# One attention and mixture-of-experts layer: chunk work spread over more units, expert results added in DRAM, experts moved from unit 38 to 44

## The reference

```
xn  = layernorm(x)                                     # 4096 tokens x 128
q, k, v = xn @ Wq + bq, xn @ Wk + bk, xn @ Wv + bv     # 16 heads of 8
attn = softmax(q k^T / sqrt(8)) v, per batch and head
logits = xn @ router_w.T                               # 8 experts
g = sigmoid(top 2 logits) / their sum
ffn = sum over the 2 chosen experts e of g_e * (silu(xn @ w_gate[e]) * (xn @ w_up[e])) @ w_down[e]
out = x + attn @ Wo + bo + ffn
```

## Time and profile before

| | |
|---|---|
| median of 3 runs | 1033.23 us (1033.08 to 1034.17) |
| the profiled execution | 1033.09 us, its span 1031.3 us |
| PE busy | 906.4 us (88%) |
| DVE busy | 684.9 us (66%), 610.4 of them in the 512 reductions of L736 |
| ACT busy | 680.3 us (66%), 538.9 of them in the exponentials of L499 |
| POOL busy | 419.3 us (41%) |
| granted clock of PE, mean | 0.894 |

### The profile page before, as it was taken

The page is one execution under the profiler, slowest core; times in us unless marked ns, Lnnn a source line. Parts: engine busy times, 40 slices in busy tenths (PEclk is TensorE's granted clock), DMA queues, the critical chain, the costliest instruction groups (busy, mean ns, idle before and its releaser), DMA issues.

```text
span 1031.3 us, 17126 instructions
## 1 busy us (share of the span) xinstructions
PE 906.4 (88%) x5469; PEld 411.0 (40%) x5469; DVE 684.9 (66%) x807; ACT 680.3 (66%) x1452; POOL 419.3 (41%) x639
## 2 busy tenths in 40 slices
PE   6275598994879999999999999999999999999870
PEld 5142233331434454444444454444444544333220
DVE  6145588883377767777777767777777677888100
ACT  2040356773448877888877887778887788787630
POOL 8454004774153222323222222222232223288786
PEclk8595558996569999999999999999999999999875
DMA  4359301233222223333333332333332222133234
GB/s 125 92 154 278 126 22 48 74 108 105 64 58 62 82 71 97 82 84 84 83 104 84 83 84 84 83 84 86 83 84 86 79 80 72 47 38 38 34 53 85
DMA packets 99354, 86.84 MB, mean 84 GB/s; under 512 B 13496, under 2 KB 86848, under 8 KB 99264
## 3 DMA queue, kind: packets, MB, share of 16 engines
q1 hardware_dynamic: 85968, 72.21, 25.2%
q0 software_dynamic: 12560, 13.39, 5.9%
q10 hardware_dynamic: 736, 0.14, 0.1%
HBM read 58.68 MB, written 26.49 MB: 83 GB/s over the span
## 4 chain that ended last, share of the span: by engine, by line
PE 67%; POOL 10%; issue 7%; ACT 6%; DVE 5%; DMA 2%; SPq 2%; POOLq 0%; ACTq 0%; DVEq 0%
PE ps L896 21%; PE ps L879 20%; PE ps L868 9%; PE ps L933 7%; POOL slots L385 6%; ACT probs L499 5%; PE ps L919 5%; POOL x_sb L423 3%; PE ps L909 2%; POOL probs L361 1%; DVE maxima L736 1%; PE ps L923 1%; DMA qk<-m_rows 1%; DVE m_parts L746 1%; DVE attn L759 1%
## 5 line engine op out<-in xcount | busy, mean ns | idle before, releaser
L736 DVE TENSOR_REDUCE maxima<-ps 128x1 f32<-128x1024 f32 x512 | 610.4, 1221 | 251.7 <-PE ps L879 250.7
L499 ACT ACTIVATE probs<-ps 128x512 f32<-128x512 f32 x1024 | 538.9, 604 | 150.8 <-PE ps L868 150.6
L868 PE MATMUL ps<-qk 36*128 36x512 f32 x1024 | 399.0, 475 | 31.0 <-DMA qk<-m_rows 18.7
L879 PE MATMUL ps<-qk 34*128 34x512 f32 x1024 | 356.9, 457 | 31.6 <-issue 22.6
L896 PE MATMUL ps<-probs,v_all 128*9 128x512 f32 x2048 | 286.9, 635 | 0.0
L879 PEld LDWEIGHTS ps<-qk 34*128 34x128 f32 x1024 | 166.1, 197 | 254.7 <-DVE maxima L736 135.2
L403 POOL TENSOR_TENSOR gxu<-gu 128x256 f32<-128x256 f32 x72 | 52.5, 730 | 419.8 <-ACT gu L535 419.8
L868 PEld LDWEIGHTS ps<-qk 36*128 36x128 f32 x1024 | 171.6, 194 | 112.1 <-ACT probs L499 85.1
L423 POOL DMA_INDIRECT x_sb<-results,slot x64 | 99.2, 1549 | 34.1 <-issue 18.0
L385 POOL DMA_INDIRECT slots<-x_sb,slot x64 | 61.4, 960 | 89.2 <-DVE x_sb L730 70.0
L933 PE MATMUL ps<-xg_T,gu_w 128*128 128x128 f32 x576 | 83.6, 290 | 0.1
(11 more groups left out here) (124 smaller groups left out, 463.0 us busy)
## 6 DMA issues: line engine op xcount, KB each, us to landing
gu_w<-L_ffn_w_gate SPq DMA_DIRECT2D x72, 128.0 KB, 2.1
gu_w<-L_ffn_w_up SPq DMA_DIRECT2D x72, 128.0 KB, 2.2
dn_w<-L_ffn_w_down SPq DMA_DIRECT2D x72, 128.0 KB, 2.1
qk<-q_parts SPq DMA_DIRECT2D x128, 64.0 KB, 2.7
qk<-k_parts SPq DMA_DIRECT2D x128, 64.0 KB, 2.7
k_parts<-probs SPq DMA_DIRECT2D x24, 256.0 KB, 3.2
slots<-y_acc POOLq DMA_DIRECT2D x9, 528.0 KB, 11.4
xg<-slots SPq DMA_DIRECT2D x72, 66.0 KB, 2.1
```

Of the source, the lines that this page charges most:

```text
L499: act.activation(probs[:, u % NPB, q, h, :], ps[:, s_bank(j), :], ACT.Exp).then_inc(s_read, 1)
L736: dve.tensor_reduce(maxima[:, p % 2, qt, h:h + 1], ps[:, x_bank(i):x_bank(i) + 2, :].rearrange("p a k -> p (a k)"), AX.X, ALU.max, negate= ...
L868: pe.matmul(ps[:, bank, :], t[r, 1, kt * P:(kt + 1) * P], t[r, 0, q * CH:(q + 1) * CH], start=True, stop=True).then_inc(s_filled, 1)
L879: mm = pe.matmul(ps[:, x_bank(i) + k, :], t[r, 0, qt * P:(qt + 1) * P], t[r, 1, k * CH:(k + 1) * CH], start=True, stop=True)
```

## The change

- Expert results: `store_result`, the 64 gathers and POOL's sums go. A DRAM tensor `acc` of 128 + 4096 rows is filled with x by two SP DMAs at unit 4. The scattered rows carry a fifth extra column with their row number in `acc` (XW 132 to 133). After `hidden(t)` POOL adds tile t - 1 to `acc` with one accumulating indirect DMA, each waiting for the one before it to land. At the end SP loads `acc` in 4 DMAs into `x_sb`, DVE adds the output bias (in units 252 to 255) and adds it to `y_acc`. The reload of x and the bias addition on POOL go.
- Chunks: the staging tiles `qk_st`, `hi_st`, `lo_st` are their own, and ACT's wait for all stores goes. `xnT` holds all chunks. Turns of chunks 2 to 7 stand in units -11 to -6, each with the logits of its chunk two steps later; q, k and v of a chunk take two units (q of chunk 7 in unit -1, its k and v in unit 0). All these jobs share the three score-side banks. The lower parts of chunks 0 and 1 are DVE's, and the norms of chunks 2 to 7 are ACT's.
- SP issues `load_pair` of pairs 0 to 2 ahead of chunk 2's stores, pair 3 at unit 0. POOL issues the zeroing of the slots as soon as pair 0 has landed.
- Routing takes units -4 to 7, its ranks are taken after unit 0.
- Experts: cluster c stands in unit 44 + 11c/4, the last in unit 244.

```diff
-FF0 = 38
+FF0 = 44
-    return FF0 + 5 * c // 2
+    return FF0 + 11 * c // 4
+for _c in REST:
+    for _job, _step in (("turn", 4 * (_c - 2)), ("lg", 4 * (_c - 2) + 2), ("q", 8 * (_c - 2) + 3), ("k", 8 * (_c - 2) + 5),
+                        ("v", 8 * (_c - 2) + 7)):
+        CHUNK_AT.setdefault((_step // 4 - LX, _step % 4), []).append((_job, _c))
+UPPER_AT = {2 * (c - 2) + 1 - LX: c for c in REST}
+LOGITS_AT = NC - 2 - LX
+ROUTE_AT = {r - 4: r for r in range(12)}
+SUM_AT = {U - 4 + b: b for b in range(B)}
+RANKS_AT = 0
...
+            for p in range(NQ - 1):
+                load_pair(p)
             for u in UNITS:
-                if u >= KT and u % KT == 0 and u // KT + NQ - 1 < NP:
+                if u - 1 in UPPER_AT:
+                    store_parts(UPPER_AT[u - 1])
+                if u >= 0 and u % KT == 0 and u // KT + NQ - 1 < NP:
                     load_pair(u // KT + NQ - 1)
+                if u == 4:
+                    sp.dma_start(acc_dram[P:P + T, :], x.rearrange("b s e -> (b s) e")).then_inc(acc_set, 16)
+                    sp.dma_start(acc_dram[0:P, :], x[0, 0:P, :]).then_inc(acc_set, 16)
...
+            pool.wait_ge(qk_in[0], LOADS)
             pool.wait_ge(zeros_ready, 1)
             for k in range(TILES // 8):
                 pool.dma_start(pieces[k], zeros).then_inc(zeros_stored, 16)
+            for c in REST:
+                lower(c)
...
+            def add_result(t):
+                pool.wait_ge(s_read, s_full("rows", t + 2))
+                if t == 0:
+                    pool.wait_ge(acc_set, 32)
+                else:
+                    pool.wait_ge(added, 16 * t)
+                pool.indirect_dma_start(out=acc_dram, out_offset=bass.IndirectOffsetOnAxis(ap=ids[:, t % 4:t % 4 + 1], axis=0),
+                                        in_=result[:, t % 3, :], in_offset=None, compute_op=ALU.add).then_inc(added, 16)
             for t in range(TILES):
                 gate_of(t)
                 hidden(t)
+                if t >= 1:
+                    add_result(t - 1)
+            add_result(TILES - 1)
...
-            upper(0)
-            dve.wait_ge(std_ready, 2)
-            dve.reciprocal(mom[:, 1, NT // B:NT], mom[:, 4, NT // B:NT]).then_inc(rstd_ready, 2)
-            upper(1)
+            statistics(1)
+            upper(0)
+            statistics(2)
+            upper(1)
+            statistics(3)
...
-                if u == 0:
-                    for c in range(NC):
-                        act.wait_ge(parts_stored[c], 80)
```

More of the change, by code:

```diff
@@ L126, in build @@
         probs = sb("probs", [P, NPB, 2, 2, CH])
[L127 to L130, removed]
+        qk_st, hi_st, lo_st = (sb(n, [P, 2, 2, CH]) for n in ("qk_st", "hi_st", "lo_st"))
         gu_w = sb("gu_w", [P, 2, 2, F])
@@ L325, in _ @@
             n = NT // B
+            sp.wait_ge(added, 16 * TILES)
+            for b in range(B):
+                sp.dma_start(x_sb[:, b * n:(b + 1) * n, 0:E],
+                             acc_dram[P + b * S:P + (b + 1) * S, :].rearrange("(m p) e -> p m e", p=P)).then_inc(acc_in[b], 16)
             for b in range(B - 1):
@@ L470, in take_chunk, with norm, take_turn @@
-            def take_chunk(c):
-                s = c % 2
+            def norm(c):
+                if c == REST[0]:
+                    act.wait_ge(rstd_ready, 2)
+                for j in range(TPC):
+                    n = c * TPC + j
+                    act.activation(x_sb[:, n, 0:E], x_sb[:, n, 0:E], ACT.Identity, scale=mom[:, 1, n:n + 1],
+                                   bias=mom[:, 5, n:n + 1]).then_inc(xn_rest, 1)
+            def take_turn(c):
+                j = S_NO["turn", c]
+                act.wait_ge(s_filled, j + 1)
+                act.activation(xnT[:, c, :], ps[:, s_bank(j), :], ACT.Copy).then_inc(s_read, 1)
@@ L562, in _ @@
                 for n, (_, _, h, q) in enumerate(STEPS):
+                    for job in CHUNK_AT.get((u, n), ()):
+                        take_chunk_job(*job)
                     if n == 2 and u in CL_AT:
@@ new lines, in turn_norm, with project, project_v @@
+                bank = s_room(S_NO["turn", c])
+                for j in range(TPC):
+                    mm = pe.transpose(ps[:, bank, j * P:(j + 1) * P], x_sb[:, c * TPC + j, 0:E], ident[:, :])
+                mm.then_inc(s_filled, 1)
+            def project(job, c, weights):
+                pe.wait_ge(s_read, s_full("turn", c))
+                bank = s_room(S_NO[job, c])
+                pe.matmul(ps[:, bank, :], weights[:, :], xnT[:, c, :], start=True, stop=True).then_inc(s_filled, 1)
+            def project_v(c):
+                bank = s_room(S_NO["v", c])
+                for j in range(TPC):
+                    mm = pe.matmul(ps[:, bank, j * E:(j + 1) * E], xnT[:, c, j * P:(j + 1) * P], wv[:, :], start=True, stop=True)
+                mm.then_inc(s_filled, 1)
@@ new lines, in logits, with chunk_job @@
+            def logits(c):
+                pe.wait_ge(s_read, s_full("turn", c))
+                for n in range(c * TPC, (c + 1) * TPC):
+                    mm = pe.matmul(ps[:, 7, n * NE:(n + 1) * NE], xnT[:, c, (n - c * TPC) * P:(n - c * TPC + 1) * P], rw_cols[:, :],
+                                   start=True, stop=True)
+                mm.then_inc(lg_ps, 1)
+            def chunk_job(job, c):
+                if job == "turn":
+                    turn_norm(c)
+                if job == "lg":
+                    logits(c)
+                if job == "q":
+                    project("q", c, wq)
+                if job == "k":
+                    project("k", c, wk)
+                if job == "v":
+                    project_v(c)
```

258 lines of the change are left out of this document (115 added, 143 removed).

## The result

The kernel after takes 973.05 us (median of four runs, 971.94 to 1033.59; the kernel before in the same session 1033.7). The ratio is 0.9407, with a 95% interval of 0.9388 to 0.9425. So it is faster by 6%, where 10% was forecast, and 931 with its range up to 955 missed it. The profiled execution took 972.98 us with a span of 971.3. It is compared with the profiled 1033.09 of before, whose span is 1031.3.

A forecast was written before the change was run, and what follows sets the result against it. Stages had different limits: DVE paced plain units at 2.76 us, PE added 1.52 per cluster. Savings 12.0 + 32.1 + 36.5 + 23.9 = 104.5 off 1033.09 gave 928.6, plus 2.4 for DMA: 931 us (0.76), range 914 to 955.

The forecast's parts named there:

- Start, -12.0: Up to the first reduction: chunk 1's last store at 23.4, first reduction at 33.5 instead of 45.48; 12.0 us saved.
- Units -11 to 12, -32.1: Chunk and routing units: 28 us for seven units, then 49.4 and 13.8; 91.2 instead of 123.35 us.
- Units -4 to 7, 49.4: Routing units: DVE sets the pace with reductions, routing parts, upper parts and ranks, 49.4 us in all.
- Units 8 to 12, 13.8: Units after the routing: five at 2.76 us each, 13.8 us.
- Experts' start, -36.5: Units 37 on: scatters end near 194, before unit 42 at 205, so PE's stall, half clock and POOL's addition go; 36.5 us saved.
- The adds, cost 0: Expert stage: accumulating DMAs land in 3.3 us, their chain needs 3.6 of 9.1 us per tile; no cost.
- The end, -23.9: After the last projection: the last sum no longer waits for gathered rows and ends at 1002.7, not 1026.62; 23.9 us saved.
- (1) DMA: Rival: DMA limits the start, stores land behind the zero fill and units wait; about 944 us, chance 0.12.
- (2) The low clock: Rival: the clock stays low after the routing, units 8 to 43 take up to 4.26 us each; 983 us, chance 0.07.
- (3): Rival: the adds set the experts' pace, 1116 us if one takes 11.4 us to land; chance 0.03.
- (4): Rival: scatters still end after unit 42, PE stands again and 15 us of low clock follow; 945 us, chance 0.02.

The follow-up runs named there:

- f4: Kernel after plus the bridge and two throwaway matmuls per head in units -11 to 2; units -11 to -5 took 41.0 us, unit 0 at 106.2.
- e2: Kernel after with all chunks' logits moved to unit -5; unit 0 at 98.8 us, 16.4 us earlier.
- e3: Kernel after with each chunk's q, k, v and logits packed into one unit with the next chunk's turn; unit 0 at 89.5 us, unit 10 at 128.9.
- g4: Kernel after unchanged, repeated in a disturbed group; its trace has units 13 to 43 at 132.1 us and a standstill in units 11 and 12.
- c1: Kernel after unchanged, repeated as yardstick; 970.85, 971.56, 1029.56 and 1035.71 us.
- e5: Kernel after with the accumulating DMAs replaced by a small POOL memset; three higher-clock runs had median 972.0 us, against 971.2 for c1; two others 1031.26 and 1031.99.
- e7: Packed chunk jobs of e3 plus the throwaway matmuls of the bridge; unit 10 at 125.9 us, all four runs 995.7 to 998.9 us.
- the bridge: Kernel after plus 52 throwaway identity matmuls in PE's idle gaps, 28 after the output bias and 24 ahead of unit -11; unit 0 at 105.7 us (115.2 without).
- g1: Kernel after plus the bridge and throwaway matmuls per head: two to unit -5, four in -4 to 3, one in 4 to 13; unit 0 at 110.3 us.

## Why the prediction was wrong

- **Start, -12.0: right in kind, 1.9 short.** The stores go out at 23.11 and 23.91, close to the 23.4 taken, but the first load at 27.72, 1.4 us later than the 26.3 that the old distance gave.
- **Units -11 to 12, -32.1: wrong, +10 measured.** The step that failed is "The clock was low for the first 7 us of this stage before, so I price one and a half units at the double: 28 us for seven". All seven ran at 0.51 and took 56.5, which is 28.5 of the 42 us. Of the forecast's 28, some 23 were work at the full clock and 5 the low clock (8.5 times its own 3.4 to 3.6 us is 29 to 31, so the sum was also a little low). Measured, the work at the full clock is about 34.5 (f4 less its fillers) and the low clock costs the other 22. So some 17 us of the miss are the clock and some 11 the pieces: `find_max` and logits at 2.7 us a unit instead of 1.2. I carried over the number of low units, although the change rearranges this work. Before, with packed units, the seven took 40.8 us, and this is the window of their full clock:

```profile
51.00:85.00 34.00, 25.98 (x109) 14.31 (x108) 14.93 (x19) 14.68 (x40) 16.31 (x16) 0.90 0.56 169
```

  That the spread order with the logits in it is what kept the clock low is shown by e2 and e3, one trace each, and by the kernel after, at 0.50 throughout these units on record and in g4, and nearly so in c1. Why the chip grants one level or the other is open.
- **Units -4 to 7, 49.4: right for another order.** e3 took 49.3. In the kernel after, q, k and v of the last chunks still lie in these units, at half clock, and it took 58.1. "DVE is the limit" held only once PE had nothing left of the chunks.
- **Units 8 to 12, 13.8:** priced at the full clock, though the earlier trace rows shows 0.50 up to 160 in the kernel before. 18.7 us measured; before it was about 21.
- **Experts' start, -36.5: right (-39.1).** The scatters end 17 us ahead of unit 42, and a cluster costs (531.3 - 441.8) / 58.2 = 1.54 us, 1.52 before. POOL has 264.08 / 58.2 = 4.5 us of work per tile, 4.7 was worked out; the gate operation behind an add takes 0.88 us, and 0.28 in the kernel before (L393), a term that the forecast left out.
- **The adds, cost 0: right**, by e5 and by 3.5 us to land.
- **The end, -23.9: right but 2.8.** The clock was at 0.50 from 927.3 to 961.4; that this makes the 2.8 isn't shown. The four sums of the bias and of `acc` on DVE (1.2 us each) are covered.
- **Rivals.** (1) DMA: no, 199 GB/s in the kernel after, and e3 went faster at 295. (2) The low clock: it was given 0.07 for units 8 to 43, and occurred, by their mean clock, in one of the four runs of the result, in two of four of c1, and in all of e7. With three such runs among eight, a median at the low clock was well possible, so the total of 973 is partly luck. Its price per unit was right (1.52 us, 1.5 forecast). It was looked for one stage too late as well, since a low clock made most of the miss in units -11 to 10. The rule of the Trainium skill that was set against it ("TensorE: Matmul & The Clock Gate", Part 1: activity releases the throttle) does not agree with these runs, as far as the profile's busy time is activity: 35.00 busy us of 35.00 at 0.50, and 132.50 of 132.50. (3) and (4) did not occur.

## What to carry to other kernels

Before pricing rearranged PE work at the full clock, look at which of its stretches ran at which clock, and price every unit of a rearranged stretch at both. Here order alone was worth 26 us by unit 0, and a total forecast needs the half-clock case as a case of its own. Price a matmul where it will stand: four `find_max` take 0.8 us in a row and 1.9 apart, at the same clock. A matmul with eight columns is not cheap: a chunk's four cost as much as two `find_max` apart, and spreading such pieces does not hide them where PE is the limit. And an earlier finish of one stage can be lost in the next: the packed order wins 30 us by unit 10 and loses 47 after it, so no version that beats the kernel after came out of these runs.

## What the runs showed of the hardware

- The granted clock has two lasting levels for one and the same stream of matmuls. Attention units without experts stay at 0.50 for 132.5 us with PE busy in all of them (e7), and at 1.00 for 91 us (the kernel after). Which one is kept differs between runs of one kernel and makes some 60 us in the total (971 and 1030 to 1036), 47 of them in units 13 to 43.
- With the bridge the clock fell from 1.00 to 0.50 at 47.4 while PE was busy in 11.88 of 11.90 us. That a wait of PE comes ahead of a fall is not so here.
- Four maxima matmuls (34 rows, 512 columns, float32) took 0.74 us in a row and about 0.47 each apart, at 1.00 in both cases (e3, g1). Four of 128 rows and 8 columns took 0.95 to 1.05 us at 1.00 and 1.88 at 0.50.
- An accumulating indirect DMA of 128 rows into DRAM took 1.66 us to issue and 3.5 to land, about as the same kind into SBUF did in the earlier trace rows.
- In three of the four groups of experiments, 64 scatters of POOL came with a stand of the other engines, some 70 us in g4, at an unchanged pace of the scatters. Whatever it is, it isn't seen on POOL's own rows.
